# A graph attention kernel: the first four row groups centred only, and the order of work in the first pass

## The reference

```python
def _layernorm(x, axis=-1, eps=1e-05):
    m = jnp.mean(x, axis=axis, keepdims=True)
    v = jnp.var(x, axis=axis, keepdims=True)
    return (x - m) / jnp.sqrt(v + eps)
...
        Wh = h @ W
        a1, a2 = (a[:Fout, 0], a[Fout:, 0])
        f1 = Wh @ a1
        f2 = Wh @ a2
        e = jax.nn.leaky_relu(f1[:, None] + f2[None, :], negative_slope=ALPHA)
        e = jnp.where(adj == 0, -jnp.inf, e)
        attention = jax.nn.softmax(e, axis=1)
        h_prime = attention @ Wh
...
    h = jnp.maximum(_layernorm(x, axis=-1), 0.0)
    x = x + _L0_gnn_ref(h, adj, L0_gnn_W, L0_gnn_a)
    return x
```

## Time and profile before

| | us |
|---|---|
| median of 3 runs | 810.08 |
| lowest and highest | 810.04, 810.56 |
| the profiled execution | 810.9 |
| its span | 809.2 |
| PE busy in the span | 785.9 (97%) |
| DVE busy | 740.8 (92%) |
| ACT busy | 483.5 (60%) |
| POOL busy | 419.2 (52%) |

### The profile page before, as it was taken

One profiled execution on the slowest core, in us unless ns is written; L12 is line 12 of the kernel. 1 busy time (PEld: TensorE's weight loads), 2 busy tenths in 40 slices (PEclk: granted clock), 3 DMA queues, 4 the chain that ended last, 5 costly groups with the idle time before them and its releaser, 6 DMA issues.

```text
span 809.2 us, 22590 instructions
## 1 busy us (share of the span) xinstructions
PE 785.9 (97%) x8969; PEld 718.5 (89%) x8969; DVE 740.8 (92%) x1189; ACT 483.5 (60%) x777; POOL 419.2 (52%) x621
## 2 busy tenths in 40 slices
PE   5899999999999999999999999999999999999997
PEld 4778799999999999999999999999999999999986
DVE  6997899999999999999999999999999999999996
ACT  6788865655655565565555556565555656555542
POOL 7687755544545554454545445454544545454320
PEclk9999999999999999999999999999999999999999
DMA  9998899999999999999999999999999999998200
GB/s 172 169 106 85 79 108 114 110 96 107 85 101 95 97 91 88 110 85 101 91 100 91 87 110 86 101 88 104 90 88 107 89 100 86 106 90 87 27 14 17
DMA packets 48321, 75.99 MB, mean 94 GB/s; under 512 B 4768, under 2 KB 13600, under 8 KB 48288
## 3 DMA queue, kind: packets, MB, share of 16 engines
q0 software_dynamic: 43008, 67.13, 87.8%
q1 hardware_dynamic: 4864, 8.39, 3.1%
q10 hardware_dynamic: 416, 0.07, 0.0%
HBM read 272.70 MB, written 4.19 MB: 342 GB/s over the span
## 4 chain that ended last, share of the span: by engine, by line
PE 90%; issue 3%; ACT 2%; DVE 2%; POOL 2%; DMA 1%; ACTq 0%; POOLq 0%; DVEq 0%
PE acc L392 53%; PE acc L396 27%; PE stage L382 7%; PE stage L365 2%; DVE wt_ring L811 1%; PE stage L373 1%; ACT ht L542 1%; DMA a_sb<-in_L_gnn_a_dram 1%; PE stage L349 1%; POOL xn L248 0%; ACT wh L549 0%; POOL tmp L267 0%; POOL masks L224 0%; POOL masks L239 0%; ACT tmp L562 0%
## 5 line engine op out<-in xcount | busy, mean ns | idle before, releaser
L811 DVE SCALAR_TENSOR_TENSOR wt_ring<-stage,packed,marks 128x512 f32<-128x512 f32 x1024 | 697.6, 743 | 54.1 <-PE acc L396 42.5
L392 PE MATMUL acc<-pairs,wt_ring 128*128 128x258 f16 x4096 | 718.9, 274 | 2.4 <-DVE pairs L801 1.3
L396 PE MATMUL acc<-pairs,wt_ring 128*128 128x129 f16 x4096 | 697.4, 219 | 0.0
L392 PEld LDWEIGHTS acc<-pairs,wt_ring 128*128 128x128 f16 x4096 | 396.0, 97 | 56.7 <-DVE pairs L801 2.2
L571 ACT ACTIVATE marks<-stage 128x1024 uint16<-128x1024 uint8 x256 | 262.0, 1023 | 290.5 <-PE stage L382 289.3
L396 PEld LDWEIGHTS acc<-pairs,wt_ring 128*128 128x128 f16 x4096 | 399.5, 98 | 2.5
L239 POOL TENSOR_TENSOR masks<-masks 128x256 int32<-128x256 int32 x256 | 184.2, 734 | 240.4 <-ACT masks L591 239.6
L214 POOL DMA_DIRECT2D masks<-in_adj_dram x240 | 130.3, 545 | 99.5 <-PE stage L382 77.5
L591 ACT ACTIVATE masks<-masks 128x512 uint16<-128x512 uint16 x256 | 158.9, 622 | 0.5 <-DMA masks<-in_adj_dram 0.5
L382 PE MATMUL stage<-ident,masks 128*128 128x128 f32 x512 | 99.2, 276 | 1.5 <-POOL masks L239 0.9
L382 PEld LDWEIGHTS stage<-ident,masks 128*128 128x128 f32 x512 | 53.0, 141 | 6.4 <-issue 2.8
(11 more groups left out here) (60 smaller groups left out, 143.9 us busy)
## 6 DMA issues: line engine op xcount, KB each, us to landing
masks<-in_adj_dram POOLq DMA_DIRECT2D x256, 256.0 KB, 7.4
out_dram<-xm SPq DMA_DIRECT2D x15, 256.0 KB, 7.2
xm<-in_x_dram SPq DMA_DIRECT2D x1, 1536.0 KB, 13.4
xm<-in_x_dram SPq DMA_DIRECT2D x1, 1024.0 KB, 10.5
xm<-in_x_dram SPq DMA_DIRECT2D x1, 768.0 KB, 5.8
xm<-in_x_dram SPq DMA_DIRECT2D x1, 512.0 KB, 7.6
xm<-in_x_dram SPq DMA_DIRECT2D x1, 256.0 KB, 3.2
out_dram<-xm SPq DMA_DIRECT2D x4, 64.0 KB, 2.6
```

The source lines that it names most:

```text
L392: return nc.tensor.matmul(acc[:, r, 0:2 * E1], wtv[:, w, r, 1, :], pairv[:, t, :, 0:E1], start=st, stop=end)
L396: return nc.tensor.matmul(acc[:, r, 0:E1], wtv[:, w, r, 0, :], pairv[:, t, 0, 0:E1], start=False, stop=False)
L811: nc.vector.scalar_tensor_tensor(out=wtq[:, t % NW], in0=e_row, scalar=packed[:, t, 1:2], in1=edges[:, k], op0=ALU.max, op1=ALU.mult).then ...
```

## The change

Six edits.

1. Groups 0 to 3 are only centred (x minus mean), on DVE for groups 0 to 2 (`centre`, four operations each) and on POOL for group 3. ACT and POOL have no normalise for them. `keep` of these groups moves from ACT to DVE, where it multiplies by 1/deviation as it copies: eight operations of 128x260 from PSUM. `inverses` leaves out its fourth operation for the two batches in question, now groups 0, 1 and groups 2, 3. x is loaded as group 0, group 1, groups 2 and 3, then as before.
2. a is loaded as two rows of 128 values, then turned by one matmul on PE and copied by ACT into `a_sb`.
3. The first `spread` reads `packed` in place; the copy L850 is gone.
4. POOL issues two of the ten adjacency parts ahead of building the identity.
5. In the steps, x_transposes(b+3) comes after quarter 0 in place of quarter 1, and relu(b+3) ahead of root and keep(b+2, 1). Ahead of the steps the same order is taken.
6. DVE's first_weights(0) to (2) have the keeps of the next group among them.

```diff
-    BATCHES = [(0, 1), (1, 4), (4, 6), (6, 10), (10, 16)]
+    LOADS = [(0, 1), (1, 2), (2, 4), (4, 6), (6, 10), (10, 16)]
+    BATCHES = [(0, 2), (2, 4), (4, 6), (6, 10), (10, 16)]
+    CENTRED = 4
...
-            for u in range(EARLY):
+            load_part(0)
+            load_part(1)
+            nc.gpsimd.memset(ident[:], 0.0).then_inc(s["ident_zero"], 1)
...
+            for u in range(2, EARLY):
                 load_part(u)
...
-            normalise(2)
-            normalise(3)
+            centre(3)
...
+            nc.tensor.matmul(acc[:, 2, 0:2], a_row[:], ident[0:2, 0:2], start=True, stop=True).then_inc(s["at_ready"], 1)
...
             features(0, 1, bank=0)
+            x_transposes(1)
             pe.wait_ge(s["norms_ready"], 1)
             transposes(0, 0)
-            x_transposes(1)
-            pe.wait_ge(s["e_ready"], 1)
-            spread(1)
+            pe.wait_ge(s["packed_ready"], 1)
+            spread(1, first=True)
...
                     if b + 2 < NQ and k == 0:
                         features(b + 2, 0)
-                    if b + 3 < NQ and k == 1:
+                    if b + 3 < NQ and k == 0:
                         x_transposes(b + 3)
...
+            act.wait_ge(s["at_ready"], 1)
+            nc.scalar.activation(a_sb[:], acc[:, 2, 0:2], ACT.Copy).then_inc(s["a_kept"], 1)
...
                 for u in SECONDS.get(b, (b + 3,)):
                     second(u // UN, u % UN)
+                if b + 3 < NQ:
+                    relu(b + 3)
                 if b in ROOTS:
                     root(ROOTS[b])
+                if CENTRED <= b + 2 < NQ:
+                    keep(b + 2, 1)
...
-                if b + 3 < NQ:
-                    relu(b + 3)
...
+            def centre(g):
+                if g >= 2:
                     dve.wait_ge(s["xt_ready"], g - 1)
+                for r in range(PACK):
                     t = g * PACK + r
                     ins = nc.vector.tensor_scalar(xn[:, g % 2, r * P:(r + 1) * P], xm[:, g, r * P:(r + 1) * P],
+                                                  stats[:, t, 1:2], None, ALU.subtract)
                 ins.then_inc(s["xn_dve"], 1)
+
+            def keep(g, h, bank=None):
+                dve.wait_ge(s["whp_ready"], 2 * g + h + 1)
+                fresh = stage[:, 3, :] if bank is None else acc[:, bank, :]
+                t = g * PACK + 2 * h
+                rstd = small[:, 5, t:t + 2].rearrange("p (r o) -> p r o", o=1)
+                nc.vector.tensor_tensor(wh[:, t:t + 2, :], fresh.rearrange("p (r c) -> p r c", r=2)[:, :, 0:WC],
+                                        rstd.to_broadcast([P, 2, WC]), ALU.mult).then_inc(s["wh_first"], 1)
...
-                weights(1, b, range(0, HALF if b == 0 else PACK))
-                low_part(b)
-                if b == 0:
+                if b + 1 < CENTRED:
+                    weights(1, b, range(0, HALF))
+                    keep(b + 1, 0)
+                    low_part(b)
+                    keep(b + 1, 1)
                     weights(1, b, range(HALF, PACK))
+                else:
+                    weights(1, b)
+                    low_part(b)
...
             statistics(0)
-            moments(0)
-            inverses(0)
-            normalise(0)
-            statistics(1)
+            centre(0)
...
+            statistics(1)
+            moments(0)
+            centre(1)
+            inverses(0)
             statistics(2)
+            keep(0, 0)
             statistics(3)
             moments(1)
+            keep(0, 1, bank=0)
+            pack(0)
+            centre(2)
             inverses(1)
-            normalise(1)
-            pack(0)
-            dve.wait_ge(s["packed_ready"], 1)
-            nc.vector.tensor_copy(e_next[:], packed[:, 0:PACK, 0]).then_inc(s["e_ready"], 1)
```

More of the change, by code:

```diff
@@ L134, in gat_kernel @@
         s = {n: sem(n) for n in (
-            "w_loaded", "a_loaded", "x_loaded0", "x_loaded1", "x_loaded2", "x_loaded3", "x_loaded4",
+            "w_loaded", "a_loaded", *(f"x_loaded{k}" for k in range(len(LOADS))),
             "adj_loaded0", "adj_loaded1", "adj_loaded2", "adj_loaded3",
@@ L149, in gat_kernel @@
         first_loaded = [s[f"first_loaded{k}"] for k in range(UN)]
-        x_loaded = [s[f"x_loaded{k}"] for k in range(len(BATCHES))]
+        x_loaded = [s[f"x_loaded{k}"] for k in range(len(LOADS))]
         x_dram = x.rearrange("(q p s) d -> p q (s d)", p=P, s=PACK)
@@ L186, in _ @@
             load_x(1)
-            for k, part in ((2, 0), (3, 1), (4, 3)):
+            load_x(2)
+            for k, part in ((3, 0), (4, 1), (5, 3)):
                 sp.wait_ge(first_loaded[part], 16)
@@ L367, in features, with spread @@
                 mm.then_inc(s["whp_ready"], 1)
-            def spread(bank):
+            def spread(bank, first=False):
                 for r in range(PACK):
-                    mm = nc.tensor.transpose(stage[:, bank, r * P:(r + 1) * P],
-                                             e_next[:, r:r + 1].to_broadcast([P, P]), ident[:])
+                    column = packed[:, r, 0:1] if first else e_next[:, r:r + 1]
+                    mm = nc.tensor.transpose(stage[:, bank, r * P:(r + 1) * P], column.to_broadcast([P, P]), ident[:])
                 mm.then_inc(s["rowp_ready"], 1)
@@ L526, in normalise @@
             def normalise(g):
[L528 to L532, removed]
-                    mm = nc.scalar.activation(xn[:, g % 2, r * P:(r + 1) * P], xm[:, g, r * P:(r + 1) * P],
-                                              ACT.Identity, scale=small[:, 5, t:t + 1], bias=small[:, 6, t:t + 1])
-                mm.then_inc(s["xn_ready"], 1)
+                act.wait_ge(s["ln_ready"], batch_of(g) - 1)
+                act.wait_ge(s["xt_ready"], g - 1)
+                t = g * PACK
+                nc.scalar.activation(xn[:, g % 2, 0:P], xm[:, g, 0:P], ACT.Identity, scale=small[:, 5, t:t + 1],
+                                     bias=small[:, 6, t:t + 1]).then_inc(s["xn_ready"], 1)
             def relu(g):
@@ L639, in _ @@
                                  accum_out=lim[:, 2:3]).then_inc(s["norms_ready"], 1)
+            relu(0)
             root(0)
-            normalise(0)
-            relu(0)
+            second(0, 0)
             root(1)
-            second(0, 0)
-            keep(0, 0)
-            keep(0, 1, bank=0)
             exponentials(0)
+            relu(1)
             unpack(0, 0, first=True)
-            normalise(2)
-            relu(1)
             high_part(0)
             second(0, 1)
-            keep(1, 0)
-            keep(1, 1)
             exponentials(1)
+            relu(2)
             unpack(1, 1, first=True)
-            relu(2)
-            normalise(3)
             for b in range(UN):
@@ L744, in statistics @@
             def statistics(g):
[L746 to L747 removed]
+                for k, (lo, hi) in enumerate(LOADS):
+                    if lo == g:
+                        dve.wait_ge(x_loaded[k], 16)
                 for r in range(0, PACK, 2):
```

67 lines of the change are left out of this document (38 added, 29 removed).

## The result

The changed kernel takes 815.86 us (median of 4 runs, 815.16 to 816.23) against 810.32 (810.04 to 810.75): ratio 1.0067, 95% interval 1.0053 to 1.0081. It is 5.5 us slower; 815.5 was forecast. Its profiled execution took 816.13, with a span of 814.4.

A forecast was written before the change was run, and what follows sets the result against it. PE bounds the kernel, so its exit from the first pass decides. Start +3.2 us, +3.75 by step 3's features, nine steps +2.0, together +5.7, less 0.26 for relu: +5.4, forecast 815.5 us, range 811.0 to 818.5.

The forecast's parts named there:

- the milestone of step 12: End of the second half of PE's features in step 12, at 84.25 us before; forecast +5.7 us.
- POOL's ring: In the steps, features, exponentials, scaled, normalise and transposes wait on each other: 5.14 us a step against 4.92.
- The start: Work up to low_part of group 3, at 35.09 us before: DVE's longer queue delays it by 3.2 us.
- Centring and its meeting with POOL: In the start, six more 128x128 operations on DVE, 1.6 us, and waiting for POOL's scaled(0), 0.7 us.
- The upper bound of +5: Start's loss if every operation of centre(2) and of the inverses waits for one of POOL's four.
- Relu ahead: In the steps, removes PE's 0.26 us wait for relu; credited with 0.26 us in step 13.
- Adjacency parts: Two parts loaded ahead of the identity: worth nothing, at the worst 0 to 0.5 us of bandwidth.
- a and the copy: In the start, W times a 1.2 us sooner and 0.7 us of copy saved, both spent on DVE's queue.
- rival B: DVE's new work in the start is all hidden and steps give 0.26 each: -4.5 us, 805.6; chance 0.08.
- A: In the steps POOL's `xn` is not late and PE's steps cost 4.54 us: +1.1, 811.2; chance 0.13.
- C: More idle time puts PE at 1.2 GHz for a further stretch: +1 to +3 us; 0.19 together with D.
- D: In the start a lands no sooner, so the start costs +4.4 us: 816.7; 0.19 together with C.

The follow-up runs named there:

- a_xt_k1: The changed kernel with x_transposes(b+3) back behind quarter 1, relu still ahead: 810.52 us.
- b_xt0: The kernel before with only the transposes of `xn` moved behind quarter 0, relu left behind unpack: 814.05 us.
- a_pool_swap: The changed kernel with normalise(b+4) ahead of scaled(b+2) on POOL in the steps: 810.17 us.
- b_best: The kernel before with a in two rows, first spread in place, the new order of the steps, and POOL's normalise ahead of scaled: 808.18 us.
- b_new_steps: The kernel before with only the two edits in the steps (transposes behind quarter 0, relu ahead): 813.90 us.
- b_parts: The kernel before with two adjacency parts issued ahead of the identity: 810.19 us.
- a_keep_act: a_xt_k1 with the eight keeps of groups 0 to 3 on ACT and the division by the deviation left out: 809.08 us.
- b_a_spread: The kernel before with a loaded in two rows and the first spread read in place: 810.29 us.
- b_relu: The kernel before with relu(b+3) ahead in the steps, the transposes still behind quarter 1: 809.71 us.

## Why the prediction was right, and where it was not

The sign, the size and the two causes hold: the time is 0.4 us from the forecast, and the milestone of step 12 was put at +5.7 and came at +5.55. Point by point:

- **POOL's ring.** Shown from three sides: it goes with the moved line (a_xt_k1), comes with it alone (b_xt0), and is cut by POOL's order (a_pool_swap). Its size was 5.14 in the sum and is 5.26 to 5.27. A slip of 0.02 is in the addition: the terms as written make 5.16. The term mis-sized is from the transposes to the end of the features: 1.73 predicted, 89.80 - 87.97 = 1.83 measured. I took durations from the old places: four transposes took 0.66 after a wait in place of 0.61, and the features behind products 0.66 to 0.67 in place of 0.61 behind transposes. The second is not the wait's doing, for in b_best, which has no wait there, they take 0.66 as well. Over nine steps slip and term make 1.1 us too little.
- **The start.** Predicted +3.2 at low_part of group 3, measured +2.23, inside the bounds of +1.8 and +5. Two terms were too large. The keep takes 0.427 us, but the sum needs the time from its start to the next one's, which was put at 0.42 and is 0.33 to 0.34 (29.35 to 29.68): eight are 2.7 us and not 3.4. Centring and its meeting with POOL were put at 1.6 + 0.7 us more on DVE. Its twelve operations took 0.90 + 0.87 + 1.56 us, and the six of normalise before took 2.13, so they are 1.2 us more; the meeting itself cost 0.7, as predicted. On the other side stand operations that the sum had at no extra cost, such as the moments at 33.95, 0.81 in place of 0.26 us; this part is not worked out in full. The features of step 3 were put at 43.7 (+3.75) and came at 42.46 (+2.50). This is 1.25 us too much, so that the two errors nearly cancel; that the total is right to 0.4 us is in part luck.
- **DVE and POOL at their shared port.** The Trainium skill (SBUF — State Buffer, "Who interferes with whom") has a DVE instruction in a two-port mode and a GpSimd instruction exclude each other for a whole instruction. The trace of the changed kernel agrees for the first centring of group 2, 0.886 us against 0.271 at best, beside scaled(0). It does not agree for what follows: DVE's next three ran through beside POOL's first centring, so that its four took 1.56 us. Nor did POOL pay for this in full: its first took 0.68 us, the other three 0.59, and two of these ran after DVE's centring was over (from 14.60). So 0.59 us looks like what this operation takes on POOL without a meeting, more than the 0.44 of normalise, and the meeting cost POOL some 0.09. The upper bound of +5 rested on turns that were not taken.
- **Relu ahead** was credited with 0.26 us in step 13 and the wait is gone; from step 12 to step 13 it is 3.92 in place of 4.41 us, 0.49. In the steps before, it is worth nothing beside POOL's ring (b_xt0 against b_new_steps: 814.05 and 813.90).
- **Adjacency parts**: 0, and so it is (b_parts).
- **a and the copy**: the product with a came at 5.55 in place of 7.05 (1.2 us were predicted). The 1.2 and 0.7 us were said to be spent on DVE's queue. They don't reach the first weights in the changed kernel, but the keeps are not the reason: in a_keep_act, with none on DVE, the exponentials of group 0 still end at 12.37 and the first weights start at 14.79. There the keeps stand on ACT behind a root that waits until 10.78 for DVE's statistics. That they would be worth something by themselves, which I wrote down for b_a_spread and which stands behind rival B, is not borne out.
- **Rivals.** A (POOL's `xn` not late) is refuted by the waits, 7.3 us in eleven. Its 4.54 us for PE's step is not a lower limit either, for b_best has steps of 4.34: the busy time of before holds longer instructions too, among others the features at 0.71 us behind their wait. B (faster) would have needed keeps of 0.2 us. C (the clock): the window of 26 to 28 us had 0.50 before and 1.00 in the changed kernel, the opposite of what C says; going by b_parts the stretch of before hid some 0.6 us of the start's loss in the milestones from step 3 on. D: a landed in time.

## What to carry to other kernels

An instruction that shows no wait can have a slack that the views of waits don't show; read it as the distance from the end of what it needs to its own start (here 0.44 us) before moving it forward, by 0.68 us in this case. Then close the ring: if what it needs depends on a result of the same step, the loss comes back in every step. And an engine that is full is the wrong place for an eviction, even when this takes the root off the path: eight keeps of 0.43 us cost 1.4 us at the end, on an engine that had been idle for 2.4 us in the same stretch.

## What the runs showed of the hardware

- A 128x260 multiply from PSUM to SBUF on DVE takes 0.427 us, with 0.33 to 0.34 to the next operation's start; `weights`, a maximum and a multiply on 128x512, takes 0.74.
- When DVE and POOL both had centring operations queued, DVE's second to fourth ran through at some 0.27 us and POOL's first took 0.68 in place of 0.59. In a_pool_swap POOL's normalise took 1.81 in place of 1.30 us, while low_part ran on DVE; low_part beside POOL's scaled took 1.14 us in the changed kernel, 1.43 in b_relu and 1.51 in a_keep_act, against 0.68.
- 1 KB for a, as 256 separate values, kept its matmul waiting until 7.05 us; as two rows of 512 bytes it was used at 4.13, issued at the same time, 1.31 us.
- PE at the 1.2 GHz level showed up in the first pass of two of the fourteen profiled executions, before (26 to 30 us) and b_relu (38 to 42 us). It did not in b_parts, whose work on PE is that of before, nor in the changed kernel, which was busy for 8.96 of the 12 us from 26 to 38, less than b_relu with 9.14. No run here tells in advance which execution has one.
